# One x1 scratch tensor read through views: kept batches gathered four at a time, each reloaded batch by itself

## The reference, cut to what matters

```python
def _gn(v, G=32, eps=1e-05):            # group norm: 32 groups of 12 channels, no affine part
    g = v.reshape(B_, G, C_ // G, H_, W_)
    return ((g - mean(g)) / sqrt(var(g) + eps)).reshape(v.shape)

x = x + displace(_gn(x), offset)        # 48 offsets, one for each 8 channels
x = x + hadamard_1x1(_gn(x))            # 384 channels padded to 512, times H512, cut to 384
```

## Time and profile before

| | us |
|---|---|
| median of 3 runs (lowest, highest) | 284.46 (283.58, 286.48) |
| the profiled execution | 283.06 |
| its span, first to last instruction | 281.4 |

### The profile page before, as it was taken

One profiled execution on the slowest core, in us unless ns is written; L12 is line 12 of the kernel. 1 busy time (PEld: TensorE's weight loads), 2 busy tenths in 40 slices (PEclk: granted clock), 3 DMA queues, 4 the chain that ended last, 5 costly groups with the idle time before them and its releaser, 6 DMA issues.

```text
span 281.4 us, 2494 instructions
## 1 busy us (share of the span) xinstructions
PE 156.2 (56%) x742; PEld 98.1 (35%) x742; DVE 201.3 (72%) x313; ACT 128.3 (46%) x189; POOL 35.7 (13%) x52
## 2 busy tenths in 40 slices
PE   0000000054971698299700589999988982899710
PEld 0000000044961698299600524444333331243200
DVE  0899999986761892577530337999999980899950
ACT  1003999929810410131000199988886603993000
POOL 0000000000000563335433600000000220000000
PEclk9999999999985599779955558999999997599995
DMA  5999999999991168997640662139999999457798
GB/s 183 417 409 409 410 409 410 311 374 410 300 250 36 23 170 195 244 279 212 146 145 22 212 273 96 76 112 408 345 360 375 390 365 402 172 233 292 292 404 346
DMA packets 25278, 76.80 MB, mean 273 GB/s; under 512 B 7368, under 2 KB 7624, under 8 KB 25048
## 3 DMA queue, kind: packets, MB, share of 16 engines
q1 hardware_dynamic: 18928, 67.07, 66.8%
q0 software_dynamic: 5504, 9.51, 10.6%
q10 hardware_dynamic: 832, 0.05, 0.2%
HBM read 67.07 MB, written 29.99 MB: 345 GB/s over the span
## 4 chain that ended last, share of the span: by engine, by line
DMA 48%; DVE 25%; issue 7%; ACT 6%; PE 4%; SPq 2%; POOL 2%; POOLq 1%; DVEq 0%; ACTq 0%
DMA ring<-x_pad 28%; DVE ring L908 14%; DMA stat_rows<-blk_stat 6%; DVE parts L264 6%; DMA ring<-x_from,row_at 6%; DMA blk<-x_pad 5%; DMA out<-ring 4%; ACT blk L500 3%; ACT parts L508 2%; PE ps L555 2%; POOL x_from L273 2%; PE ps L542 1%; DVE blk L264 1%; PE ps L533 1%; DVE blk L814 1%
## 5 line engine op out<-in xcount | busy, mean ns | idle before, releaser
L614 PE MATMUL ps<-parts,had_sb 128*128 128x512 f16 x216 | 56.2, 398 | 6.8 <-DVE parts L264 4.4
L908 DVE SCALAR_TENSOR_TENSOR ring<-ps,beta,ring 128x1024 f32<-128x1024 f32 x48 | 59.6, 1273 | 0.0
L542 PE MATMUL ps<-geo_sb,blk 128*128 128x128 f32 x72 | 13.6, 357 | 71.5 <-DMA blk<-x_pad 56.7
L555 PE MATMUL ps<-parts 128*128 128x64 f32 (+4 forms) x306 | 42.1, 305 | 6.5 <-ACT parts L454 6.4
L555 PEld LDWEIGHTS ps<-parts 128*128 128x128 f32 x306 | 41.5, 219 | 7.2 <-ACT parts L454 6.8
L264 DVE TENSOR_TENSOR parts<-blk,parts 128x1024 f16<-128x1024 f32 x27 | 32.7, 1213 | 15.3 <-ACT parts L508 15.3
L753 DVE BATCH_NORM_STATS2 halfstat<-ring 128x6 f32<-128x512 f32 x64 | 38.9, 670 | 4.9 <-DMA ring<-x_pad 4.9
L500 ACT ACTIVATE blk<-ring,gn 128x1024 f32<-128x1024 f32 x32 | 37.7, 1227 | 0.0
L624 PE MATMUL ps<-ring,first_w 128*128 128x512 f32 x64 | 34.4, 664 | 5.7 <-ACT first_w L492 5.7
L542 PEld LDWEIGHTS ps<-geo_sb,blk 128*128 128x128 f32 x72 | 11.6, 189 | 72.0 <-issue 65.3
L614 PEld LDWEIGHTS ps<-parts,had_sb 128*128 128x128 f16 x216 | 20.6, 101 | 44.4 <-DVE parts L264 12.4
(11 more groups left out here) (109 smaller groups left out, 125.5 us busy)
## 6 DMA issues: line engine op xcount, KB each, us to landing
ring<-x_pad SPq DMA_DIRECT2D x20, 1536.0 KB, 15.3
out<-ring SPq DMA_DIRECT2D x13, 1536.0 KB, 7.3
blk<-x_pad SPq DMA_DIRECT2D x18, 512.0 KB, 8.2
out<-ring SPq DMA_DIRECT2D x9, 512.0 KB, 5.2
x_from<-blk POOLq DMA_DIRECT2D x9, 288.0 KB, 4.1
x_from<-blk POOLq DMA_DIRECT2D x9, 128.0 KB, 4.8
x_from<-blk POOLq DMA_DIRECT2D x9, 96.0 KB, 3.9
geo_sb<-geo SPq DMA_DIRECT2D x1, 683.0 KB, 4.7
```

Source lines behind the costliest of these rows:

```text
L542: last = pe.transpose(pixels[:, j // 4, 128 * (j % 4):128 * (j % 4 + 1)], shifted[:, 128 * j:128 * (j + 1)], eye)
L555: last = pe.matmul(sums[:, bank, 32 * (a - 16 * bank):32 * (b - 16 * bank)], pixels[:, j, :], weights[:, a - (4 * j - 1):b - (4 * j - 1), ...
L614: last = pe.matmul(ps[n % 4][:, h, :], had_sb[:, sign, :], part_of(n, t, part)[:, 512 * h:512 * (h + 1)], start=False, stop=ends and part ...
L908: dve.scalar_tensor_tensor(ring[:, m, place_of(i), :], ps[n % 4][:, :, :].rearrange("p a n -> p (a n)"), beta[:, i % BATCH:i % BATCH + 1], ...
```

## The change

There is one scratch tensor, `x1_rows`, with a row of 16 images (64 KB) for each channel, in place of three tensors of 3, 9 and 4 images a row. A block is written to it with one DMA instead of three. It is read through views: with rows of `count` images, the row number of a channel in a view is `row * 16 / count + first / count`, so DVE makes seven lists of row numbers (one instruction each, after the fast path's parameters). The 12 batches that stay in `ring` are gathered as (4, 4), (8, 4), (12, 4), where it was (4, 3) and (7, 9). Each of the four reloaded batches has a semaphore of its own and is gathered with three instructions of its own once its reload has landed; before, POOL waited for all four reloads and gathered them together. ACT waits for a group at n = 0, 4, 8, 12, 13, 14 and 15, where it did at n = 0, 3 and 12.

```diff
-PARTS = ((4, 3), (7, 9), (0, 4))
+PARTS = [(4, 4), (8, 4), (12, 4)] + [(j, 1) for j in range(EXTRA)]
+KEPT = 3
...
-        def rows_out(eng, row, count, tile, sem):
-
-            for first, count in PARTS:
-                eng.dma_start(x1_part[first][row, :].rearrange("c (b n) -> b c n", n=PIXELS),
-                              tile[BIND * first:BIND * (first + count), :]).then_inc(sem, 16)
-
-        def gather_rows(eng, first, count, limit, signal):
-
-            rows, at = x1_part[first], place_of(first + BATCH) if first < EXTRA else place_of(first)
+        def gather_part(eng, n, limit, signal):
+
+            first, count = PARTS[n]
+            at = place_of(first + BATCH) if first < EXTRA else place_of(first)
+            runs = x1_rows[0:limit, :].rearrange("c (g n) -> (c g) n", n=count * PIXELS)
             for t in range(CT):
                 eng.indirect_dma_start(ring[:, t, at:at + count, :].rearrange("p b n -> p (b n)"), None,
-                                       rows[0:limit, :], bass.IndirectOffsetOnAxis(ap=row_at[:, t:t + 1], axis=0),
-                                       bounds_check=limit - 1, oob_is_err=False).then_inc(signal, 16)
+                                       runs, bass.IndirectOffsetOnAxis(ap=row_at[:, n, t:t + 1], axis=0),
+                                       bounds_check=limit * BATCH // count - 1, oob_is_err=False).then_inc(signal, 16)
...
-                sp.dma_start(ring[:, :, j, :], x_bcp[j]).then_inc(reload_done, 16)
+                sp.dma_start(ring[:, :, j, :], x_bcp[j]).then_inc(reload_done[j], 16)
...
-                rows_out(pool, slice(BIND * k, BIND * (k + 1)), BIND, blk[:, u, :], blk_out[u])
+                pool.dma_start(x1_rows[BIND * k:BIND * (k + 1), :].rearrange("c (b n) -> b c n", b=BATCH), blk[:, u, :]).then_inc(blk_out[u], 16)
...
+            pool.wait_ge(rows_ready, 1)
             with pool.If(active > FAST):
...
-            for part, (first, count) in enumerate(PARTS[0:2]):
-                gather_rows(pool, first, count, FAST * BIND, patch_done[part])
-            pool.wait_ge(reload_done, 16 * EXTRA)
-            first, count = PARTS[2]
-            with pool.If(active > FAST):
-                gather_rows(pool, first, count, CHANNELS, more_patched)
-                pool.wait_ge(more_patched, 16 * 3 * CT)
-            gather_rows(pool, first, count, FAST * BIND, late_patch_done)
+            for n in range(KEPT):
+                gather_part(pool, n, FAST * BIND, part_in[n])
+            for j in range(EXTRA):
+                pool.wait_ge(reload_done[j], 16)
+                with pool.If(active > FAST):
+                    gather_part(pool, KEPT + j, CHANNELS, more_patched)
+                    pool.wait_ge(more_patched, 16 * CT * (KEPT + j + 1))
+                gather_part(pool, KEPT + j, FAST * BIND, part_in[KEPT + j])
...
-            act.wait_ge(patch_done[0], 16 * CT)
             for n in range(BATCH):
-                if n == PARTS[0][1]:
-                    act.wait_ge(patch_done[1], 16 * CT)
-                if n == RING:
-                    act.wait_ge(late_patch_done, 16 * CT)
+                part = n // EXTRA if n < RING else KEPT + n - RING
+                if n % EXTRA == 0 or n >= RING:
+                    act.wait_ge(part_in[part], 16 * CT)
...
+            for n, (first, count) in enumerate(PARTS):
+                last = dve.tensor_scalar(row_at[:, n, :], row_f[:, 0, :], float(BATCH // count), float(first // count), ALU.mult, ALU.add)
+            last.then_inc(rows_ready, 1)
```

More of the change, by code:

```diff
@@ L111, in build @@
     ds = bass.ds
-    x1_part = {first: nc.dram_tensor(f"x1_from{first}", [CHANNELS, count * PIXELS], FP32).ap() for first, count in PARTS}
+    x1_rows = nc.dram_tensor("x1_rows", [CHANNELS, BATCH * PIXELS], FP32).ap()
     stat_rows = nc.dram_tensor("stat_rows", [CHANNELS, BATCH * 2], FP32).ap()
@@ L145, in build @@
         row_f = sb("row_f", [128, 2, CT])
-        row_at = sb("row_at", [128, CT], INT32)
+        row_at = sb("row_at", [128, len(PARTS), CT], INT32)
         halfstat = sb("halfstat", [128, 4, CT - 1, 2, 6])
@@ L220, in build @@
         store_done = [sem(f"store_done{u}") for u in range(2)]
-        reload_done = sem("reload_done")
-        patch_done = [sem(f"patch_done{part}") for part in range(2)]
-        late_patch_done = sem("late_patch_done")
+        reload_done = [sem(f"reload_done{j}") for j in range(EXTRA)]
+        rows_ready = sem("rows_ready")
+        part_in = [sem(f"part_in{n}") for n in range(len(PARTS))]
         stat_patched = sem("stat_patched")
@@ L306, in fetch_plain @@
                 if k >= DEEP:
-                    sp.wait_ge(blk_out[k % DEEP], 64 * (k // DEEP))
+                    sp.wait_ge(blk_out[k % DEEP], 32 * (k // DEEP))
                 sp.dma_start(blk[:, k % DEEP, :],
@@ L342, in _ @@
                 for u in range(DEEP):
-                    sp.wait_ge(blk_out[u], 64 * blocks_in(u))
+                    sp.wait_ge(blk_out[u], 32 * blocks_in(u))
                 with sp.Fori(FAST, OFFSETS) as k:
@@ L354, in _ @@
                     sp.wait_ge(more_ready, m + 1)
-                    rows_out(sp, ds(k * BIND, BIND), BIND, blk[:, 0, :], more_out)
+                    sp.dma_start(x1_rows[ds(k * BIND, BIND), :].rearrange("c (b n) -> b c n", b=BATCH), blk[:, 0, :]).then_inc(more_out, 16)
                     sp.dma_start(stat_rows[ds(c_at, BIND), :].rearrange("c (b k) -> b c k", k=2), blk_stat[:, 0, :]).then_inc(more_out, 16)
@@ L415, in _ @@
             with pool.If(active > FAST):
-                pool.wait_ge(more_out, 64 * (OFFSETS - FAST))
+                pool.wait_ge(more_out, 32 * (OFFSETS - FAST))
             pool.dma_start(stat[:, :, :, :].rearrange("p t b k -> p t (b k)"),
                           stat_rows.rearrange("(t c) n -> c t n", t=CT)).then_inc(stat_patched, 16)
+            pool.wait_ge(rows_ready, 1)
             with pool.If(active > FAST):
-                for first, count in PARTS[0:2]:
-                    gather_rows(pool, first, count, CHANNELS, more_patched)
-                pool.wait_ge(more_patched, 16 * 2 * CT)
-            for part, (first, count) in enumerate(PARTS[0:2]):
-                gather_rows(pool, first, count, FAST * BIND, patch_done[part])
-            pool.wait_ge(reload_done, 16 * EXTRA)
-            first, count = PARTS[2]
-            with pool.If(active > FAST):
-                gather_rows(pool, first, count, CHANNELS, more_patched)
-                pool.wait_ge(more_patched, 16 * 3 * CT)
-            gather_rows(pool, first, count, FAST * BIND, late_patch_done)
+                for n in range(KEPT):
+                    gather_part(pool, n, CHANNELS, more_patched)
+                pool.wait_ge(more_patched, 16 * CT * KEPT)
+            for n in range(KEPT):
+                gather_part(pool, n, FAST * BIND, part_in[n])
[5 more added lines that the diff above has]
+                gather_part(pool, KEPT + j, FAST * BIND, part_in[KEPT + j])
         @block.scalar
@@ L859, in _ @@
                 for u in range(DEEP):
-                    dve.wait_ge(blk_out[u], 64 * blocks_in(u))
+                    dve.wait_ge(blk_out[u], 32 * blocks_in(u))
                 with dve.Fori(FAST, OFFSETS) as k:
@@ L880, in _ @@
                     dve.bn_aggr(blk_stat[:, 0, :], blk_half[:, 0, :, :].rearrange("p h s -> p (h s)")).then_inc(more_ready, 1)
-                    dve.wait_ge(more_out, 64 * m + 64)
+                    dve.wait_ge(more_out, 32 * m + 32)
                     dve.memset(scrap[:, 3:4], 0.0)
```

4 lines of the change are left out of this document (2 added, 2 removed).

## The result

The changed kernel took 271.06 us, the median of four runs (269.05 to 275.77), beside 284.02 for the kernel before; the ratio is 0.951, interval 0.939 to 0.962. In a second set on another occasion it was 0.939 (0.931 to 0.946), with single runs from 265.3 to 274.3. The ratio and its interval are of the fast runs alone, those within 1.5% of the fastest of the same kernel, while the median is of all. The single runs of the kernel before lie within 3.2 us in each of these two sets (and within 6.4 and 7.2 us in two later ones), those of the changed kernel within 6.7 and 8.9.

What follows compares the result with a forecast made beforehand. Stage 5 was taken as bound by DVE except for one hole, stage 2 by a loop of latencies. -9.2 - 1.7 + 0.5 + 0 = -10.4 us gave 272.7 profiled, 274.1 as a median; range 271.0 to 280.0.

Steps and rivals of the forecast that it cites:

- The hole: Stage 5, n = 12: DVE stands 9.2 us because batch 0's gather waits for batch 3's reload; it closes, -9.2 us.
- Gather 3: Gather of the last reloaded batch, in by 239.1 us; DVE does not feel it before 245.0, 5.9 us to spare.
- The store queue: Stores worked off during the hole have less time; the queue fits with 2.2 us left: 0 us, at worst 2.
- The rival in which the stores take the gain back: Stage 5: small pieces or mixed reads cost DMA 5%, 4 us; about 275.7, as a median 277; chance 0.07.
- More gathers beside a busy DVE: Twelve late gathers instead of three while DVE works: DVE charged nothing, POOL up to 1 us per group.
- One row write: Stage 2, blocks 0, 5 and 8: the moments' write is issued 0.52, 0.79 and 0.41 us sooner, -1.7 us.
- The bound of 3 us: Upper bound on the gain from one row write; the lower bound was no gain at all.
- The first gather: Before the product: four batches instead of three, 0.295 MB more at 378 GB/s; +0.5 us, bounds -0.3 to +1.8.
- The slower rival: Rows 64 KB apart make the one tensor slower to write and read; 290 if times double; chance 0.09.
- The signs: Forecast wrong if a gather releases ACT at n = 13 to 15, last store starts over 10 us late, or moments' landing exceeds 7.
- The chances: Forecast 0.76; faster by more than 1% 0.90, within 1% 0.05, slower 0.05.
- The forecast's own range: Whole kernel: 271.5 to 276, from the bounds of the row write, the first gather and the store queue.

Runs made afterwards that it cites:

- the other execution of the changed kernel: The changed kernel run again without an edit; profiled at 268.12 us, median of six 268.96 us, 0.939 of before.
- the experiments with three and with one: The changed kernel with three row writes a block, cut by batches (274.12 us) or pixels (272.9 us); with one write and late gathers together, 280.13 us.
- tensors of their own: The kernel before with groups cut (4, 4), (8, 8), (0, 4), each with its own tensor, three writes a block: 285.61 us, 1.015 of before.
- late gathers apart: The kernel before with each reloaded batch gathered by itself after its own reload; three row writes and groups (4, 3), (7, 9) stay: 277.06 us, 0.972.
- narrow writes: The changed kernel with each block written to the one tensor by three DMAs, of 3, 9 and 4 batches: 274.12 us, 0.969.
- the two with the moments on a semaphore of their own: The changed kernel with the moments' write on its own semaphore: 269.05 us alone, 265.21 with the first four batches also gathered two and two.
- The kernel with both edits: The changed kernel with the first four batches gathered two and two and the moments' write on its own semaphore: 265.21 us, 0.933.
- three wide writes: The changed kernel with each block written by three DMAs that cut the pixels, all 128 partitions in each: 272.9 us, 0.965; a further execution 272.04.
- two and two: The changed kernel with the first four batches gathered two and two instead of four together: 269.4 us, 0.951.

## Why the prediction was right and wrong

**The hole, -9.2 us: right.** From the first weights to DVE's end 109.77 became 100.47, 9.30 less. Gather 3 was to be in time with 5.9 us to spare, and no gather released ACT at n = 12 to 15.

**The store queue, 0 with up to 2: right.** The tail behind DVE kept its 10.3 us, and DMA worked at a share of 1.01 from 190 to 240. The rival in which the stores take the gain back did not happen.

**More gathers beside a busy DVE, nothing: right.** Three of the twelve late gathers on POOL took 1.9 to 2.0 us and one 1.69, the others 0.99 to 1.25 (timeline of POOL, gathers of batch 0 and one of batch 2):

```profile
193.96 0.99 POOL L277 DMA_INDIRECT ring<-x_rows,row_at  x1 [32.13 <-DMA ring<-x_pad]
195.25 1.93 POOL L277 DMA_INDIRECT ring<-x_rows,row_at  x1 [0.31 <-issue]
197.49 2.02 POOL L277 DMA_INDIRECT ring<-x_rows,row_at  x1 [0.30 <-issue]
...
218.03 0.99 POOL L277 DMA_INDIRECT ring<-x_rows,row_at  x1 [0.31 <-issue]
```

DVE beside them (timeline of DVE):

```profile
195.10 1.22 DVE L265 TENSOR_TENSOR parts<-blk,parts 128x1024 f16<-128x1024 f32 x1
...
197.43 1.22 DVE L265 TENSOR_TENSOR parts<-blk,parts 128x1024 f16<-128x1024 f32 x1
...
218.48 1.22 DVE L265 TENSOR_TENSOR parts<-blk,parts 128x1024 f16<-128x1024 f32 x1
```

DVE's low halves take 1.22 us with a gather beside them and without one (200.95). The gathers at 195.25 and 197.49 start within a low half, and both end 0.86 us after it does; so do the other four that start within one (0.86 to 0.87 us). The gather at 218.03 was under way when DVE's instruction started at 218.48, and neither took longer. The rule of the Trainium skill that was weighed there ("SBUF — State Buffer", section "SBUF: two separate sides") gives the port to whichever instruction starts first and blocks the other. The trace agrees where DVE was first; where a gather was first it shows no loss on DVE, so the loss of up to 17 us that the prediction worked out by it did not come.

**One row write, -1.7 us: the direction right, size and mechanism wrong; this is the step that failed.** The prediction let the moments' issue move by 0.52, 0.79 and 0.41 us and left the time from issue to landing at the 5.46, 6.74 and 5.24 us of before. The reverse happened: the issue hardly moved, and the landing did. POOL starts 0.66 us after DVE's moments are ready (144.54 to 145.20), not 0.28, so from DVE's result to the issue the three hops take 2.23, 2.20 and 2.20 us where they took 2.33, 2.60 and 2.22: 0.5 us in all. The landings became shorter by 1.65, 1.09 and 1.95 us, 4.7 in all.

The later load of block 6 takes back 3.9, and two terms that the prediction had at nothing, without naming them, count as well: SP's instructions ahead of that load, 1.3 us less, and block 8's load, 0.3 more. With 0.1 of the issue times that lies ahead of the first moments, that makes 2.2 of the 2.3 us by which the stretch from the first moments to the read-back is shorter. In the other execution of the changed kernel the three landings are 5.8 us shorter, the load takes back only 0.6, and the stretch is 7.2 us shorter.

The bound of 3 us that the prediction put on this gain is given there without a working, and it did not hold: the three landings alone gave 4.7 and 5.8. That a small POOL transfer can land much sooner stood in the trace of the kernel before, in its list of DMA issues (operation, count, KB, median us to landing):

```profile
stat<-stat_rows POOLq DMA_DIRECT2D x1, 48.0 KB, 2.4
```

With nothing of POOL's ahead of it the read-back landed in 2.4 us, where the moments' writes took 5.2 to 6.7. That the landing depends on the row writes ahead of it is shown by the experiments with three and with one; that it is their data that it waits for is argued.

**The first gather, +0.5 us: wrong, +2.3.** The landing took 7.21 us for 5.40, 1.8 more, which is the upper bound that the prediction gave (all of it grows by a third); 0.8 us at the rate of a full DMA system was too little. The other 0.5 us is that the scales were ready 8.41 us after the read-back's issue instead of 8.94, so the gather had less time to hide in; the prediction had nothing for that. With tensors of their own four batches were late too, so the extra bytes are enough to explain it, though nine profiles spread from 5.84 to 7.24 us.

**The slower rival**, one tensor slower to write and read, did not happen: written at the 64 KB pitch the landings are shorter than before, and a first gather of four batches from rows 16 KB apart (6.34 us) lies inside the spread of those from rows 64 KB apart. The Trainium skill's rates for far larger pitches ("DMA: Bandwidth & Descriptors", section "Latency and other measured facts") are neither borne out nor contradicted; no run here has such a pitch.

**The signs.** One that the prediction gave for itself, a moments' landing over 7 us, was met at block 2 (9.8 us). It said nothing of the terms: that landing is not in the chain, and before it took 7.8.

**The chances.** Nine tenths went to faster by over 1%, and that came. The forecast's own range, 271.5 to 276, does not follow from the bounds that it names: added up they give 272.0 to 279.1. The range given, 271.0 to 280.0, was drawn from terms of one execution each; the changed kernel spreads from 265.3 to 275.8, and most of its runs lie below 271.

## What to carry to other kernels

Give each consumer a wait for the piece it needs, in the order of need, and ask what a group of transfers waits for last: smaller gathers, each with a wait of its own, were worth 9.3 us here (5.3 of them by the waits), and the 9.2 could be read from one gap. When transfers ahead of a small one on the same queue are merged or moved, its landing can change as well as its issue, so bound the landing by a small one that had nothing ahead of it. And where a stage is a loop of landings, read its spread from several executions before drawing a range.

## What was not expected of the hardware

**PE's clock at the end of the loads.** In five of the fourteen profiles of this study the granted clock from 66 to 84 us is 0.50, the 1.2 GHz level, and not near 1: late gathers apart, narrow writes (both), and the two with the moments on a semaphore of their own. The kernel with both edits, windows of 60 to 84 us:

```profile
60.00:66.00 6.00, 0.63 (x4) 0.27 (x2) 4.86 (x12) 3.57 (x10) 0.00 (x0) 0.82 1.03 412
66.00:84.00 18.00, 17.00 (x79) 17.00 (x79) 11.68 (x37) 11.45 (x28) 0.00 (x0) 0.50 1.03 314
```

The kernel before:

```profile
60.00:66.00 6.00, 0.49 (x3) 0.09 (x1) 4.29 (x11) 3.66 (x11) 0.00 (x0) 1.00 1.02 407
66.00:84.00 18.00, 14.99 (x90) 14.90 (x91) 12.51 (x41) 11.36 (x28) 0.00 (x0) 0.94 1.04 312
```

PE is nearly idle from 60 to 66 in both; in the one the clock falls within that stretch and the convolutions that follow take 15.03 us, in the other it holds and they take 11.81. PE comes later to all that stands behind them, and the first moments of stage 2 are issued at 104.00 to 104.89 in these five, at 99.20 to 100.81 in the other nine. PE's work in that stretch does not tell which way it goes: it is 0.49 to 0.80 us where the clock held (seven profiles) and 0.44 to 1.22 us where it fell. In two of the nine (three wide writes, second profile; two and two) the clock is low only to about 78 us and stage 2 starts on time. Three wide writes is one kernel, and its first profile kept the clock, so the edit alone does not decide it.

**A dip of the DMA rate** to 25 to 82 GB/s for 2 us at a share of up to 1.23, shown above, goes with a load's landing up to 3.2 us later in some executions and is absent in others. Its cause stays open.
